# Queries and keys projected with the head's width on the partitions

## The reference, cut to what matters

```python
q = einsum('bim,ghmd->bghid', x, w_aq);  k = einsum('bim,gmd->bgid', x, w_ak);  v = einsum('bim,gmd->bgid', x, w_av)
q, k = rope(q), rope(k)      # first half of d: even*cos - odd*sin;  second half: even*sin + odd*cos
s = causal(q @ k^T / sqrt(128));  p = softmax(s);  o = p @ v
x = layernorm(x + einsum('bghid,ghdm->bim', o, w_ao))
x = layernorm(x + experts(x))      # 64 routed experts, 6 a token, and a shared one
```

## Time and profile before

| | |
|---|---|
| median of three runs | 1109.04 us |
| profiled execution | 1111.22 us |
| its span, first to last instruction | 1109.4 us |
| mean granted TensorE clock | 0.958 |
| busy TensorE / VectorE / ScalarE / GpSimd | 1006.9 / 655.8 / 524.2 / 369.2 us |
| DMA | 128.34 MB, 116 GB/s |

### The profile page before, as it was taken

One profiled execution on the slowest core, in us unless ns is written; L12 is line 12 of the kernel. 1 busy time (PEld: TensorE's weight loads), 2 busy tenths in 40 slices (PEclk: granted clock), 3 DMA queues, 4 the chain that ended last, 5 costly groups with the idle time before them and its releaser, 6 DMA issues.

```text
span 1109.4 us, 17287 instructions
## 1 busy us (share of the span) xinstructions
PE 1006.9 (91%) x5448; PEld 758.6 (68%) x5448; DVE 655.8 (59%) x1666; ACT 524.2 (47%) x1151; POOL 369.2 (33%) x407
## 2 busy tenths in 40 slices
PE   6999999799999999999998999999999998649835
PEld 4888887666778777777676667777777776526412
DVE  6777765366565576675655776474747646424326
ACT  4333334454564556464644565464645644126402
POOL 6766665223321212102133333221211111126721
PEclk9999998799999999999998999999999999869968
DMA  8445233534221111210324333441211123988687
GB/s 241 166 178 186 106 140 109 184 110 121 79 95 59 59 58 58 70 44 23 94 56 111 102 89 102 119 122 57 78 30 58 35 73 93 245 249 196 82 259 291
DMA packets 107416, 128.34 MB, mean 116 GB/s; under 512 B 16465, under 2 KB 73925, under 8 KB 107328
## 3 DMA queue, kind: packets, MB, share of 16 engines
q1 hardware_dynamic: 84688, 96.82, 28.1%
q10 hardware_dynamic: 13408, 22.09, 6.3%
q0 software_dynamic: 9232, 8.34, 4.1%
HBM read 81.99 MB, written 58.59 MB: 127 GB/s over the span
## 4 chain that ended last, share of the span: by engine, by line
PE 69%; DVE 10%; issue 7%; DMA 6%; SPq 3%; POOL 3%; ACT 2%; ACTq 0%; POOLq 0%; DVEq 0%
PE s_ps L1045 15%; PE o_ps L1072 11%; PE ring L1055 9%; PE ring L1084 9%; PE o_ps L1075 6%; PE s_ps L1016 5%; PE ring L1016 5%; DMA sums<-erow,goal_u 2%; DVE neg_max L1244 2%; SPq L709 2%; PE s_ps L1023 1%; PE s_ps L1048 1%; PE ring L1099 1%; DVE pt_lo L1182 1%; POOL sums L808 1%
## 5 line engine op out<-in xcount | busy, mean ns | idle before, releaser
L1244 DVE TENSOR_REDUCE neg_max<-s_ps 128x1 f32<-128x128 f32 (+7 forms) x256 | 191.9, 751 | 166.6 <-PE s_ps L1048 165.5
L1045 PE MATMUL s_ps<-kt,qt_hi 128*128 128x512 f32 (+3 forms) x768 | 245.0, 401 | 8.6 <-POOL qt_lo L770 6.3
L898 ACT ACTIVATE probs<-s_ps,neg_max 128x128 f32<-128x128 f32 (+7 forms) x256 | 189.7, 741 | 129.9 <-DVE neg_max L1244 127.2
L770 POOL TENSOR_TENSOR qt_lo<-q_raw,qt_hi 128x512 fp32r<-128x512 f32 x64 | 81.9, 1281 | 324.6 <-ACT qt_hi L824 324.3
L1045 PEld LDWEIGHTS s_ps<-kt,qt_hi 128*128 128x128 f32 x768 | 140.2, 195 | 64.8 <-issue 38.2
L1055 PE MATMUL ring<-ident,probs 128*128 128x128 f32 x1152 | 177.3, 277 | 6.4 <-DVE pt_lo L1182 4.5
L1072 PE MATMUL o_ps<-pt,v 128*128 128x512 f32 x336 | 174.3, 601 | 2.0 <-DVE ot L1263 1.9
L1055 PEld LDWEIGHTS ring<-ident,probs 128*128 128x128 f32 x1152 | 129.3, 143 | 37.7 <-issue 22.1
L907 ACT ACTIVATE pt<-ring 128x512 f32<-128x512 f32 x168 | 99.8, 595 | 98.4 <-PE ring L1055 97.9
L1045 PE MATMUL s_ps<-kt,qt_lo 128*128 128x512 f32 (+3 forms) x384 | 134.5, 350 | 0.0
L795 POOL DMA_INDIRECT slot_rows<-row,slot_u x96 | 94.9, 989 | 98.2 <-DVE slot_u L1367 76.0
(11 more groups left out here) (197 smaller groups left out, 1529.4 us busy)
## 6 DMA issues: line engine op xcount, KB each, us to landing
q_rows<-q_out SPq DMA_DIRECT2D x64, 256.0 KB, 2.0
q_raw<-q_rows ACTq DMA_DIRECT2D x64, 256.0 KB, 2.8
inv_row<-inverses SPq DMA_DIRECT2D x64, 256.0 KB, 3.4
fsum<-sums SPq DMA_DIRECT2D x48, 256.0 KB, 8.0
sums<-blank SPq DMA_DIRECT2D x16, 640.0 KB, 4.9
wexp<-in_L_ffn_w_gate_dram SPq DMA_DIRECT2D x32, 192.0 KB, 4.8
wexp<-in_L_ffn_w_up_dram SPq DMA_DIRECT2D x32, 192.0 KB, 5.1
wexp<-in_L_ffn_w_down_dram SPq DMA_DIRECT2D x32, 192.0 KB, 5.8
```

What stands on the lines that cost most here:

```text
L770: pool.tensor_tensor(qt_lo[:, u % 2, :], q_raw[:, u % QB, :], qt_hi[:, u % 2, :].bitcast(F32), ALU.subtract).then_inc(q_ready, 1)
L898: act.activation(probs[:, u % 2, h, 0:blocks(u) * P], s_ps[:, n % 2, score_cols(n)], ACT.Exp, bias=neg_max[:, n % 8:n % 8 + 1], accum_out= ...
L1045: pe.matmul(s_ps[:, n % 2, c + a:c + e], q[qp], k[kp][:, a:e], start=(qp == kp == 0), stop=(qp == 1 and not last))
L1244: dve.tensor_reduce(neg_max[:, n % 8:n % 8 + 1], s_ps[:, n % 2, score_cols(n)], AX_X, ALU.max, negate=True).then_inc(max_ready, 1)
```

## The change

Queries and keys come out of the projection already turned, so that no roped row is transposed. The weights are now the stationary side and 512 tokens (a chunk, `CHUNK` = 4 tiles) the moving side: a step ("proj", c, name, a, z) gives a bank of 128 partitions x 512 tokens. The weights are laid out by halves when they are split (`by_halves`), so that a bank holds the half z (even or odd) of two heads together (a = 0: heads 0 and 1; a = 1: heads 2 and 3). Even and odd of a head then lie on the same partitions of two banks. cos and sin are turned once: `tab` steps (two at chunk 0 and two at chunk 1, eight fp32 products each) put them on the partitions, once for each of the two heads, and ScalarE copies them.

VectorE multiplies each bank by cos and by sin into `prods[a]`; GpSimd combines in place, after both halves, by one subtraction and one addition of 128x512; SP stores each of the two results (256 KB, pieces of 2 KB) to `qk_rows`, whose rows are head and d, and whose columns are tokens. VectorE may write `prods[a]` again when both stores of the name before have landed (`rope_stored`). K goes the same way and is loaded back for a whole batch by two DMAs of 64 partitions, 1 MB each (`load_k`, on SP, in chunks 1 and 3), into the place of its low part; ScalarE and GpSimd split it (`ksplit`), in chunk 2 for batch 0 and in units 10, 13, 16 and 19 for batch 1. `load_q` becomes two DMAs of 64 partitions each, in pieces of 512 B.

V keeps its form (`projv`), the first chunk's four before all else. x is read four tiles ahead (`XB` = 4). Blank rows are written at the V steps 4 to 11. `wo` is loaded at the step exp (1, 1) after the projections alone, and ScalarE's first write of `pt` waits for the last rope stores. V's stored part is loaded into the place of its low part (two semaphores in turn), a unit or so later than before. `q_raw`, `qt_hi` and `qt_lo` have changed places in SBUF and are among what `load_homes` can count as free at the end of the second stage. The number of V products and of projection products is unchanged.

```diff
-XB = 2
+XB = 4
...
-HIGH_AT = {("proj", 0, "K"): ["K", 0], ("proj", 0, 0): [1], ("proj", 0, 1): [2, 3, "V"]}
-LOW_AT = {("proj", 0, "K"): ["K", 0], ("proj", 0, 0): [1], ("proj", 0, 1): [2], ("proj", 0, 2): [3],
-          ("proj", 0, 3): ["V"]}
-MISC_AT = ("proj", 1, "V")
-BLOCKS_IN_TURN = [n for names in HIGH_AT.values() for n in names]
+CHUNK = 4
+CHUNKS = TILES // CHUNK
+CW = CHUNK * P
+HT = T // CW
+
+HIGH_AT = {("xt", 2): ["V"], ("projv", 1): ["K"], ("projv", 2): [0], ("proj", 0, "K", 1, 0): [1],
+           ("proj", 0, 0, 0, 0): [2], ("proj", 0, 0, 1, 0): [3]}
+LOW_AT = {("xt", 2): ["V"], ("projv", 1): ["K"], ("projv", 2): [0], ("proj", 0, "K", 1, 0): [1],
+          ("proj", 0, 0, 1, 0): [2], ("proj", 0, 1, 1, 0): [3]}
+MISC_AT = ("projv", CHUNK)
+BLOCKS_IN_TURN = ["V", "K", 0, 1, 2, 3]
...
-    seq, roped = [("xt", 0)], []
-    for i in range(TILES):
-        for name in BLOCKS:
-            seq.append(("proj", i, name))
-            if name != "V":
-                roped.append(("qkt", i, name))
-            if len(roped) > ROPE_LAG:
-                seq.append(roped.pop(0))
-            if name == 2 and i + 1 < TILES:
-                seq.append(("xt", i + 1))
-            if (i, name) == (TILES - 1, 1):
-                seq += [("qsplit", 0), ("qsplit", 1)]
-    return seq + roped
+    seq = [("xt", i) for i in range(CHUNK)] + [("projv", i) for i in range(CHUNK)]
+    for c in range(CHUNKS):
+        for name in BLOCKS[:-1]:
+            if c % HT and name == "K":
+                seq += [("tab", c, t) for t in range(2)] if c < HT else []
+            for a in range(2):
+                if c == 0 and name == "K" and a == 0:
+                    seq += [("tab", 0, t) for t in range(2)]
+                seq += [("proj", c, name, a, z) for z in range(2)] + [("rope", c, name, a)]
+                if a == 0 and name != "K" and c + 1 < CHUNKS:
+                    seq.append(("xt", (c + 1) * CHUNK + name))
+                if (c, name, a) == (CHUNKS - 1, 2, 1):
+                    seq += [("qsplit", 0), ("qsplit", 1)]
+                if c == 2 and a == 1 and name != "K":
+                    seq.append(("ksplit", 0, name))
+            if name != "K" and c >= 1:
+                seq.append(("projv", c * CHUNK + name))
+    return seq
+
+
+KSPLIT_AT = [10, 13, 16, 19]
...
-if u // G == NT - 1:
-    seq.append(("vsplit", u % G))
+if 0 <= u - NT * G + 1 < G:
+    seq.append(("vsplit", u - NT * G + 1))
...
+if h == 1 and u in KSPLIT_AT:
+    seq.append(("ksplit", 1, KSPLIT_AT.index(u)))
...
-for h, between in enumerate(((), LAST[:2], LAST[2:3], LAST[3:])):
+for h, between in enumerate(((), LAST[:3], LAST[3:], ())):
...
-LAST = [("proj", TILES - 1, 3), ("qkt", TILES - 1, 1), ("proj", TILES - 1, "V"), ("qkt", TILES - 1, 2),
-        ("qkt", TILES - 1, 3)]
+LAST = [("proj", CHUNKS - 1, 3, 1, 0), ("proj", CHUNKS - 1, 3, 1, 1), ("rope", CHUNKS - 1, 3, 1), ("projv", TILES - 1)]
...
+def rope_turns(c, name):
+
+    return c * NAMES + BLOCKS.index(name) + 1
...
+w_two = sb("w_two", [P, 6, 2, HD * MC], F32R, pre)
+prods = sb("prods", [P, 2, 2, 2, CW], F32, pre)
...
+tab_raw = sb("tab_raw", [P, 2, NT, D // 2], F32, pre)
+tab = sb("tab", [P, 2, T], F32, pre)
+xt_hi = sb("xt_hi", [P, 2, MC, CW], F32R, pre)
+xt_lo = sb("xt_lo", [P, 2, MC, CW], F32R, pre)
...
+rows_of = qk_rows.rearrange("(n z x) t -> n z x t", n=NAMES, z=2)
+
+def rope_done(eng, c, name):
+
+    for n in range(4):
+        eng.wait_ge(rope_stored[n], 16 * rope_turns(c, name))
...
+def load_k(b):
+
+    rope_done(sp, CHUNKS // B * (b + 1) - 1, "K")
+    for z in range(2):
+        src = rows_of[0, z, :, b * T:(b + 1) * T].rearrange("(g d) t -> d g t", g=G)
+        sp.dma_start(kt_lo[b][z * D // 2:(z + 1) * D // 2, :, :].bitcast(F32), src).then_inc(k_loaded, 16)
...
-if s[0] == "qkt" and s[2] != "K":
-    u = s[1] * G + s[2]
-    read(sp, s)
-    sp.dma_start(q_rows[u * P:(u + 1) * P, :], q_out[:, u % QB, :]).then_inc(q_stored[u % QB], 16)
-if s[0] == "proj" and s[2] == "V" and s[1] >= NT + VF:
+if s[0] == "rope":
+    c, name, a = s[1:]
+    n = ROPE_AT[s[1:]]
+    for z in range(2):
+        sp.wait_ge(rot_ready, 2 * n + z + 1)
+        sp.dma_start(rows_of[BLOCKS.index(name), z, a * P:(a + 1) * P, c * CW:(c + 1) * CW],
+                     prods[:, a, z, 0, :]).then_inc(rope_stored[2 * a + z], 16)
+if s == ("proj", CHUNKS // B - 1, 1, 0, 0):
+    load_k(0)
+if s == ("proj", CHUNKS - 1, 1, 0, 0):
+    sp.wait_ge(wlo_ready, len(BLOCKS))
+    load_k(1)
...
+if s[0] == "rope":
+
+    c, name, a = s[1:]
+    read(pool, ("proj", c, name, a, 1))
+    for z, op in enumerate((ALU.subtract, ALU.add)):
+        pool.tensor_tensor(prods[:, a, z, 0, :], prods[:, a, z, 0, :], prods[:, a, z, 1, :], op
+                           ).then_inc(rot_ready, 1)
+if s[0] == "ksplit":
+    b, g = s[1:]
+    pool.wait_ge(k_hi_ready, G * b + g + 1)
+    pool.tensor_tensor(kt_lo[b][:, g, :], kt_lo[b][:, g, :].bitcast(F32), kt_hi[b][:, g, :].bitcast(F32),
+                       ALU.subtract).then_inc(k_ready, 1)
...
-if s == ("score", 1, 0):
+if s == ("exp", 1, 1):
     pool.wait_ge(proj_ready, PROJ_ALL)
-    pool.wait_ge(rot_ready, len(ROPE_AT))
-    pool.wait_ge(qkt_ready, len(QKT_AT))
-    for n in range(QB):
-        pool.wait_ge(q_stored[n], 16 * len(range(n, UNITS, QB)))
-    pool.wait_ge(v_stored, 16 * VS)
     pool.dma_start(wo[:, :, :], w_ao.rearrange("g h d m -> d (g h) m")).then_inc(wo_loaded, 16)
...
-act.wait_ge(q_stored[u % QB], 16 * (u // QB + 1))
-act.dma_start(q_raw[:, u % QB, :], q_rows[u * P:(u + 1) * P, :]).then_inc(q_loaded[u % QB], 16)
+i, g = divmod(u, G)
+rope_done(act, i // CHUNK, g)
+for z in range(2):
+    src = rows_of[1 + g, z, :, i * P:(i + 1) * P].rearrange("(h d) t -> d h t", h=H)
+    act.dma_start(q_raw[z * D // 2:(z + 1) * D // 2, u % QB, :].rearrange("d (h t) -> d h t", h=H), src
+                  ).then_inc(q_loaded[u % QB], 16)
...
+if kind == "ksplit":
+    b, g = s[1:]
+    act.wait_ge(k_loaded, 32 * (b + 1))
+    split(kt_hi[b][:, g, :], kt_lo[b][:, g, :].bitcast(F32)).then_inc(k_hi_ready, 1)
...
+if s == ("proj", CHUNKS - 1, 1, 1, 0):
+    act.wait_ge(proj_ready, PROJ_AT[("proj", CHUNKS - 1, 0, 1, 1)] + 1)
...
+if n == 0:
+    rope_done(act, CHUNKS - 1, 3)
...
+if kind == "tab":
+    pe.wait_ge(table_loaded, 32)
+    for k in range(CHUNK):
+        for half in range(2):
+            ins = pe.matmul(bank(s)[half * D // 2:(half + 1) * D // 2, k * P:(k + 1) * P],
+                            tab_raw[:, s[2], s[1] * CHUNK + k, :], ident[:, :], start=True, stop=True)
+    ins.then_inc(tab_ready, 1)
...
+a, z = s[3:]
+sides = ws[:, z, a * P:(a + 1) * P], xs
...
-if kind == "qkt":
-    n = QKT_AT[s[1:]] % 2
-    pe.wait_ge(rot_ready, QKT_AT[s[1:]] + 1)
-    for h in range(H):
-        ins = pe.transpose(bank(s)[:, h * P:(h + 1) * P],
-                           q_rot[:, n, h, :, :].rearrange("p a d -> p (a d)"), ident[:, :])
-    ins.then_inc(qkt_ready, 1)
...
+if kind == "proj":
+    c, name, a, z = s[1:]
+    turn = rope_turns(c, name) - 1
+    dve.wait_ge(proj_ready, PROJ_AT[s] + 1)
+    if z == 0:
+        used(dve, rope_stored[2 * a], 16 * turn)
+        used(dve, rope_stored[2 * a + 1], 16 * turn)
+    if a == z == 0 and c < HT and name == "K":
+        read(dve, ("tab", c, 1))
+    here = slice(c % HT * CW, (c % HT + 1) * CW)
+    dve.tensor_tensor(prods[:, a, 0, z, :], bank(s), tab[:, z, here], ALU.mult)
+    reader(dve.tensor_tensor(prods[:, a, 1, z, :], bank(s), tab[:, 1 - z, here], ALU.mult), s)
```

More of the change, by code:

```diff
@@ L206, in schedule @@
     return seq
[L209 removed]
+PRE_RINGED = ("xt", "tab", "proj", "projv")
 RINGED = ("ptrans", "outproj", "x1t", "rtr", "ht", "count", "sd")
@@ L248, with chunk_of @@
 PS_AT = {k: n for n, k in enumerate(k for k in PT_AT if k[1] >= VF)}
[L249 to L253, removed]
+PROJ_AT = {s: n for n, s in enumerate(s for s in SEQ if s[0] in ("proj", "projv"))}
+PROJ_ALL = len(PROJ_AT)
+ROPE_AT = {s[1:]: n for n, s in enumerate(s for s in SEQ if s[0] == "rope")}
+NAMES = len(BLOCKS) - 1
+def chunk_of(step):
+    return step[1] // CHUNK if step[0] == "projv" else step[1]
+def rope_turns(c, name):
+    return c * NAMES + BLOCKS.index(name) + 1
+assert all(n == 2 * (rope_turns(c, name) - 1) + a for (c, name, a), n in ROPE_AT.items())
 def build(nc, x, w_aq, w_ak, w_av, w_ao, gate_w, bias, w_gate, w_up, w_down, ws_gate, ws_up, ws_down,
@@ L433, in build @@
         v_stored = sem("v_stored")
-        v_loaded = sem("v_loaded")
+        v_loaded = [sem(f"v_loaded{n}") for n in range(2)]
         v_later_hi = sem("v_later_hi")
@@ L573, in _ @@
             load_x(0)
+            load_x(1)
             for name in BLOCKS_IN_TURN:
@@ L1007, in _ @@
                     ins.then_inc(xt_ready, 1)
-                if kind == "proj":
-                    i, name = s[1:]
-                    n = BLOCKS.index(name)
-                    read(pe, ("xt", i))
-                    pe.wait_ge(whi_ready[n], 1)
```

(29 more changed lines are left out.)

183 lines of the change are left out of this document (80 added, 103 removed).

## The result

The kernel after takes 1119.34 us in the median of four runs (1118.12 to 1121.08), beside 1109.12 (1108.13 to 1111.79) of the kernel before: a ratio of 1.0093, 95% interval 1.0077 to 1.0109. It is slower by just under 1%, clear of the noise, where faster was forecast.

The account below looks back on a forecast made before the run. The prediction took the new `prods` loop through the store's landing as the projection stage's bound. From 1111.2 us profiled, less 12.5 at unit 2's start, plus 1.5 behind it, it forecast 1100.2, median 1098, range 1088 to 1107.

Parts of the forecast that it names:

- the tail: From the last name's begin to unit 2: last ropes, last store, then ScalarE's `pt` write; about 16 us, to 188.2.
- start of the first rope: Projection start: four V blocks, tables, first K step, then VectorE's first rope at 20.4 us (11.4 before).
- That is 7.2 us: One round of a `prods` buffer: VectorE products 2.5, GpSimd 2.5, store landing 2.0, plus hand-overs; each name takes 7.2 us.
- low parts of the weights: Three low parts of weights fall into the first chunk's ropes and slow GpSimd, about 1 us each, +3.
- K's low parts beside the ropes: Chunk 2: four K splits of batch 0, 2.4 us each on GpSimd, exceed its slack of 2.2 by little, +1.
- I take 6 for the first and 5 for the second: Delay of the rope stores behind the two K loads on SP's queue, each bounded by 3.2 to 8.3 us; +11.
- the 16 us of the port rule: Alternative estimate for both K loads: 64 partitions reach half the ports, 196 GB/s, so they cost 16 rather than 11 us.
- the old hole: Between the stages before: TensorE idle from 194.3 to 200.6 as `wo`'s load waits for stores; its 6.3 us would go.
- the loop is longer than now's stage: Rival: store receipts under other SP transfers lengthen the projection loop; gain gone from 7.5 us a name, 1123 at 8.2; chance 0.14.
- TensorE-bound: Rival: TensorE stays the projection stage's bound; 1071 us fully, 1084 half way; chance 0.22.
- query loads paid by short units: Rival: behind the projections, eight short units pay 1 us each for query loads; forecast plus 8, 1106; chance 0.08.
- a hidden change: Rival: nothing moves because the tail's wait and stalls eat the whole gain; 1109; chance 0.05.

Follow-up runs that it names:

- Experiment 7: Kernel after with `qk_rows` cut by chunk, so stores have no gaps in HBM and each K load is four 64-partition DMAs: 1115.01 us.
- Experiment 3: Kernel after with two heads interleaved on the partitions, so K and query loads span all 128 partitions, same bytes and DMA count: 1111.14 us.
- Experiment 8: Kernel after with heads interleaved on the partitions and each K load cut into four 512 KB pieces behind four names' stores: 1104.7 us.
- experiment 2: Kernel after with the four K load DMAs issued on ScalarE's queue instead of SP's: 1119.22 us.
- experiment 4: Kernel after with four dead identity transposes on TensorE before each K or group step, 320 in all: 1123.58 us.
- the late slot: Kernel after with GpSimd's result written into the second step's slot, so the next name's first-step products wait for GpSimd alone: 1095.64 us.

## Why the prediction was wrong

The mechanism was right; two of its terms, a round of the loop and the price of the K loads, were too small. The forecast had VectorE waiting for the stores, TensorE with holes and not the bound, two holes behind the K loads, and the tail waiting for the last store; all four are in the trace. The forecast's start of unit 2 was at 188.2 us and came at 206.99. By its own steps, for the start of the last name (172.2 forecast, 189.27 measured):

| step | forecast | measured | difference |
|---|---|---|---|
| start of the first rope | 20.4 | 19.27 | -1.1 |
| "That is 7.2 us", 19 names | 136.8 | 19 x 7.6 = 144.4 | +7.6 |
| low parts of the weights | 3 | 3.1 | +0.1 |
| K's low parts beside the ropes | 1 | 0 (names of 7.6 to 7.7) | -1 |
| `load_k`, twice | 11 | 9.1 + 7.4 = 16.5 | +5.5 |
| not foreseen | 0 | 6 | +6 |

The start came 1.1 us early because the first sixteen products of the tables took 2.0 us, where the forecast had 3.5 us for the same step. (The forecast's 153.5 us for TensorE as the bound adds up to 153.1 by its own terms; nothing else hangs on it.)

The first step that failed is the loop's term. The products (2.5), GpSimd (2.5) and the hand-over to it (0.08) were as forecast; the store was put at the 2.0 us of stores to `q_rows` and took 2.3, and the hand-overs were 0.1 us longer. The row was of another pattern: 256 KB without gaps in HBM. Experiment 7 takes the gaps away, and the landing is 2.0 and the name 7.3, 0.1 from the forecast. Four tenths of a microsecond count because 19 names pay them: 7.6 us of a forecast gain of 11.0. By itself this doesn't turn the sign; together with the next term, 13.1 us, it does.

The second is "I take 6 for the first and 5 for the second". Of its bounds for one load, 3.2 to 8.3 us, the upper one was nearer, and the first load passed it (9.1). The row it rests on, the rate of full queues, was of DMAs over 128 partitions; these loads touch 64 and moved 223 GB/s with the DMA engines busy throughout. Experiment 3 spreads them over 128 partitions, and they cost 6.0 + 4.9 = 10.9 us, just the forecast's 11: the forecast had priced another transfer. Experiment 8, cutting them, takes 6.3 more off; experiment 2 shows that their place in the queue is nothing. The prediction had set the 16 us of the port rule aside in favour of rows that held no such transfer. The Trainium skill, page "SBUF — State Buffer", section "Door 1: The DMA port swizzle", says that partitions 0 to 63 reach half of the ports. By this rule, with its 196 GB/s, the prediction's estimate for the two loads was 16. The trace agrees: 16.5 us, at 223 GB/s for all that moved.

The 6 us not foreseen: 1.2 us for a name that VectorE spends partly on low parts of the router's and shared weights (8.8); 1.8 for the name at 118.62, which TensorE, at a lowered clock behind the first hole, brought late; 2.3 for two names of 8.4 and 9.1, whose stores landed after 3.2 to 4.0 us instead of 2.3, by their place beside a store of blank rows and one of `v_rows` (issued at 149.80 and 150.28, both landing after 5.8 us) and then beside the first query loads (from 158.81 on); no run tells this apart; the rest in tenths. That the first hole also lowers the clock and so makes a second, smaller loss was no step of the forecast.

The tail took 17.7 us where 16 was forecast: 189.27 to 206.99, in the forecast's order (score (0,0) at +2.6, the last stores issued by +12.8, `pt` at +16.7). The difference is the last store, which was put at 2.0 us and landed 3.8 us after issue, beside query loads and `v_rows`. That the old hole goes and this wait takes its place was right. TensorE stood still for 17.0 us ahead of score (0,0). Behind unit 2, 1.5 us was forecast and 2.8 came, by the span. The first output projection is already 3.0 later than unit 2; before it the exps of the third unit hold the transposes for 3.07 us (0.46 before). Query loads of 64 partitions are hidden, as forecast: even where the output projections fall 2.1 us further behind (eighth to ninth, 578 to 612 us), no wait of TensorE's ends with a query load or its split.

The sum: 172.2 + 17.1 + 16 + 1.7 gives 207.0, and with the 1.3 behind it the 20.1 us that separate the forecast change of the span (-11.0) from the measured one (+9.1).

Of the rivals, "the loop is longer than now's stage" came true, at the place that it named, the store receipts, and near its lower price: "With both K loads at their upper ends (+6) the gain is gone from 7.5 us a name". Measured were +5.5 and 7.6. TensorE-bound, query loads paid by short units and a hidden change are refuted by experiment 4, by the distances of the output projections, and by the result. A chance of 0.14 was small for it: the forecast's gain was the difference of two long terms, 137 us of loop being one, and an error of 5% in the loop undid over half of it.

## What to carry to other kernels

When a change puts a DMA's receipt into a buffer's round, the round is a new bound, whatever the engines' busy shares say: write it out as a sum, price each transfer by a row with its own pattern (gaps in HBM, partitions touched), and multiply an error of a tenth of a microsecond by the number of rounds. Ask then which part of the buffer the DMA really reads: putting the result in the part that is written last took 23.7 us off here. A large load that is needed much later can be cut in pieces behind the small stores that are needed now: 6.4 us with the store in the loop, 3.8 with the late slot. Issuing it from another queue gave nothing.

## What the runs showed of the hardware that was not expected

- A store of 256 KB in pieces of 2 KB, 8 KB apart in HBM, lands after 2.3 us; without gaps after 2.0, with the same partitions and bytes (medians between 20 and 70 us, experiment 7).
- Loads of 1 MB onto 64 partitions kept the DMA engines busy at 223 GB/s, and held up stores of all 128 partitions as long from another queue as from their own (longest wait 10.7 us with the load on either queue). Over 128 partitions the same bytes landed after 8.3 us instead of 11.3 in the median.
- Behind a hole of some 10 us on VectorE that TensorE ran dry in, the granted clock was 0.73 over 18 us; with 320 dead transposes in the kernel it was 1.00 in the same stretch, with 13.34 us busy in place of 13.09.
